# Layer-0 weight products in full fp32 instead of three split-half products

## The reference

```python
def layer0(H, W, A):
    HW = einsum('bnf,fo->bno', H, W)
    A_norm = relu((A + A.T) * 0.5)
    D = sum(A_norm, axis=1)
    d = where(D > 0, D ** -0.5, 0)
    L = eye(N) - d[:, None] * A_norm * d[None, :]
    return relu(einsum('nm,bmo->bno', L, HW))

h = maximum(layernorm(x), 0.0)
x = x + layer0(h, L0_W, adj)
h = maximum(layernorm(x), 0.0)
x = x + layer1(h, L1_W, adj, L1_bias)
```

## Time and profile before

| | |
|---|---|
| median of 3 runs | 978.55 us (977.78 to 979.16) |
| profiled execution, own time | 977.52 us |
| its span, first to last instruction | 975.8 us |
| PE busy | 936.8 us (96%) |
| DVE, ACT, POOL busy | 566.6, 503.6, 287.5 us |
| DMA | 213.73 MB, 219 GB/s on average |

### The profile page before, as it was taken

How to read it: one execution, slowest core, us unless ns; L and a number is a source line. 1 busy time by engine, 2 the same in 40 slices (tenths; PEclk the granted TensorE clock), 3 DMA queues, 4 the chain that set the end, 5 groups by cost and what they waited for, 6 DMA issues and landing times.

```text
span 975.8 us, 17599 instructions
## 1 busy us (share of the span) xinstructions
PE 936.8 (96%) x4614; PEld 796.1 (82%) x4614; DVE 566.6 (58%) x1491; ACT 503.6 (52%) x1058; POOL 287.5 (29%) x289
## 2 busy tenths in 40 slices
PE   4887899999999999999999999999999999999998
PEld 3876688888888888888888887888888888888886
DVE  5885877777777776565665655443443333343442
ACT  5986666666666665545555455433334333333331
POOL 3786143434344343443444433111111100000000
PEclk9977799999999999999999999999999999999999
DMA  8995699999999986566555564676666555555552
GB/s 235 314 327 172 191 299 306 337 313 340 326 310 340 322 285 218 162 175 193 168 171 156 182 194 143 196 217 194 192 184 192 179 168 167 165 167 166 161 164 70
DMA packets 181210, 213.73 MB, mean 219 GB/s; under 512 B 13616, under 2 KB 116016, under 8 KB 178992
## 3 DMA queue, kind: packets, MB, share of 16 engines
q1 hardware_dynamic: 138448, 159.23, 54.0%
q10 hardware_dynamic: 42720, 54.01, 15.8%
HBM read 145.04 MB, written 68.16 MB: 218 GB/s over the span
## 4 chain that ended last, share of the span: by engine, by line
PE 88%; POOL 5%; issue 4%; DMA 1%; DVE 1%; ACT 1%; SPq 0%; ACTq 0%; POOLq 0%; DVEq 0%
PE psAcc L485 23%; PE psAcc L487 23%; PE psAcc L486 23%; POOL colacc L917 3%; PE psA L387 3%; PE psG L456 2%; PE psG L458 2%; PE psG L457 2%; PE psZ L418 2%; POOL n_rs L909 1%; PE psW L359 1%; PE psW L358 1%; PE psAcc L499 1%; PE psAcc L498 1%; PE psAcc L497 1%
## 5 line engine op out<-in xcount | busy, mean ns | idle before, releaser
L545 ACT ACTIVATE Lh<-C 128x512 fp32r<-128x512 f32 x256 | 161.0, 630 | 289.7 <-PE psAcc L487 229.8
L485 PE MATMUL psAcc<-Xh,Lh 128*128 128x512 f32 x512 | 207.7, 406 | 5.6 <-DVE Xl L776 4.7
L487 PE MATMUL psAcc<-Xh,Ll 128*128 128x512 f32 x512 | 202.0, 395 | 0.0
L486 PE MATMUL psAcc<-Xl,Lh 128*128 128x512 f32 x512 | 201.3, 393 | 0.0
L485 PE MATMUL psAcc<-Yh,Lh 128*128 128x512 f32 x512 | 200.8, 392 | 0.0
L487 PE MATMUL psAcc<-Yh,Ll 128*128 128x512 f32 x512 | 200.1, 391 | 0.0
L486 PE MATMUL psAcc<-Yl,Lh 128*128 128x512 f32 x512 | 199.9, 390 | 0.0
L720 DVE TENSOR_TENSOR Ll<-C,Lh 128x512 fp32r<-128x512 f32 x128 | 91.6, 717 | 143.5 <-ACT Lh L545 143.4
L485 PEld LDWEIGHTS psAcc<-Xh,Lh 128*128 128x128 f32 x512 | 97.5, 191 | 24.5 <-issue 6.4
L487 PEld LDWEIGHTS psAcc<-Xh,Ll 128*128 128x128 f32 x512 | 97.1, 190 | 21.2
L487 PEld LDWEIGHTS psAcc<-Yh,Ll 128*128 128x128 f32 x512 | 96.1, 188 | 20.4
(11 more groups left out here) (124 smaller groups left out, 1472.1 us busy)
## 6 DMA issues: line engine op xcount, KB each, us to landing
C<-at_dram SPq DMA_DIRECT2D x128, 256.0 KB, 2.7
at_dram<-AT SPq DMA_DIRECT2D x16, 1088.0 KB, 5.5
R<-in_adj SPq DMA_DIRECT2D x64, 256.0 KB, 6.1
C<-in_adj SPq DMA_DIRECT2D x64, 256.0 KB, 5.3
s_dram<-C ACTq DMA_DIRECT2D x64, 256.0 KB, 4.5
g_dram<-g ACTq DMA_DIRECT2D x32, 512.0 KB, 3.9
C<-s_dram SPq DMA_DIRECT2D x64, 256.0 KB, 3.9
t_dram<-x ACTq DMA_DIRECT2D x32, 256.0 KB, 2.2
```

The lines of the kernel that those rows point to most:

```text
L485: mm(acc, lh, rh[:, k, :], start=k == 0, stop=False)
L486: mm(acc, lh, rl[:, k, :], start=False, stop=False)
L487: mm(acc, ll, rh[:, k, :], start=False, stop=c < L1 and k == NB - 1).then_inc(used, 1)
L545: A(Lh[:, q, :], C[:, q, :], ACT.Relu if s.c < L1 else ACT.Copy).then_inc(lhi, 1)
```

## The change

The transposed tile of `h` stays one fp32 copy, in one of four buffers that are idle in the preparation (`z`, `h2` and the two parts of `g12`). The product with W0 is one fp32 matmul per block, with W0 read as it was loaded (`x1[:, 0, 0:F]`), instead of three fp32r matmuls. The low half on DVE (`low0`) is gone, and with it the semaphore `t0lo`; `t0hi` is now `t0_ok`. ACT's copy may run three tiles ahead of the product instead of one. The second half of the batches keeps its three products (`yTh`, `yTl`).

```diff
-        T0 = [(yTh, yTl), (hTh, hTl)]
+        T0 = [z[:, :], h2[:, :], g12[:, 0, :], g12[:, 1, :]]
...
             def turn0(m):
 
                 pe.wait_ge(s0_h, m + 1)
-                wait(pe, t0hi, m - 1)
-                wait(pe, t0lo, m - 1)
+                wait(pe, t0_ok, m - 1)
...
             def times_W0(m):
 
                 if m == 0:
-                    pe.wait_ge(wlo_ok, 1)
-                pe.wait_ge(t0hi, m + 1)
-                pe.wait_ge(t0lo, m + 1)
+                    pe.wait_ge(ld_w, 32)
+                pe.wait_ge(t0_ok, m + 1)
                 wait(pe, hw0, m - 1)
-                hi, lo = T0[m % 2]
-                by_W0(psG[:, m % 2, :], hi, lo).then_inc(w0_ok, 1)
+                for b in range(HB):
+                    f = slice(b * F, (b + 1) * F)
+                    last = mm(psG[:, m % 2, f], T0[m % 4][:, f], x1[:, 0, 0:F], start=True, stop=True)
+                last.then_inc(w0_ok, 1)
...
                 if c < 2:
-                    pe.wait_ge(t0lo, NB)
+                    pe.wait_ge(t0_ok, NB)
...
                 act.wait_ge(t0, m + 1)
-                wait(act, w0_ok, m - 1)
-                A(T0[m % 2][0][:, :], psAcc[:, m % 2, :], ACT.Copy).then_inc(t0hi, 1)
+                wait(act, w0_ok, m - 3)
+                A(T0[m % 4], psAcc[:, m % 2, :], ACT.Copy).then_inc(t0_ok, 1)
...
                         act.wait_ge(wlo_ok, 1)
+                        act.wait_ge(w0_ok, NB)
...
-            def low0(m):
-                dve.wait_ge(t0hi, m + 1)
-                wait(dve, w0_ok, m - 1)
-                hi, lo = T0[m % 2]
-                V.tensor_tensor(lo[:, :], psAcc[:, m % 2, :], hi[:, :].bitcast(F32), ALU.subtract).then_inc(t0lo, 1)
-
...
-                        if m >= 3:
-                            low0(m - 3)
-            low0(NB - 1)
```

More of the change, by code:

```diff
@@ L169, in build @@
         prep_hi, prep_lo, gpre_lo = sems("prep_hi", "prep_lo", "gpre_lo")
-        t0, t0hi, t0lo, w0_ok, hw0 = sems("t0", "t0hi", "t0lo", "w0_ok", "hw0")
+        t0, t0_ok, w0_ok, hw0 = sems("t0", "t0_ok", "w0_ok", "hw0")
         yT, yThi, yTlo, yw_ok = sems("yT", "yThi", "yTlo", "yw_ok")
```

## The result

| | before | changed |
|---|---|---|
| median of 6 runs | 977.14 us (975.75 to 979.16) | 971.37 us (969.78 to 973.06) |
| ratio, 95% interval | | 0.994 (0.9924 to 0.9957) |
| span of the profiled execution | 975.8 us | 969.1 us |

The kernel is faster by some 5.8 us, 0.6%. When the changed kernel was timed again beside the first experiments, the ratio was 0.9954 (0.9937 to 0.9971), 4.5 us. Single executions of one kernel lie 3 to 4 us apart.

A forecast was written before the change was run, and what follows sets the result against it. Only the preparation, to about 98 us, could gain, with PE full afterwards and no engine full throughout before. 3.4 us by the ring plus 0.86 us at its end gave 4.3 us: 978.55 to 974.3 us, range 971.5 to 977.6 us.

The forecast's parts named there:

- (a): PE, per node tile: four fp32 matmuls replace twelve, eight records, costing 0.9 us less slow and 0.5 us less fast.
- (b): DVE: sixteen low halves removed, 16 x 0.68 = 10.9 us, worth only what somebody waited for.
- the five waits behind the low half: 43 to 75 us: ACT waits at five stages for `sring`, which stands behind the low half on DVE; 2.6 us to gain.
- 17 to 29 us: Early preparation: product starts 1.28 us sooner and is shorter, so ACT becomes last; 2.4 us taken of 2.7 us idle.
- The cap by the loads: Last column strip in the preparation: its landing limits the ring's 5.0 us gain to 3.3 to 5.3 us; 3.4 us taken.
- The ring: Tiles passed round five parties in the preparation: 5.0 us of waits to gain, 3.4 us taken because of the loads.
- The 3.0 us by bytes: 17 to 29 us: how much sooner loads could come, from 253 against 336 GB/s, instead of 1.0 us by DMA share.
- Rival 1: Preparation: loads or POOL hold the ring, worth only 1.3 us there, 976.4 us; chance 0.23 together with the clock rival.
- The end of the preparation: Last node tile's products, before `Xh`: eight records save 0.86 us at the slow clock, all of it on the path.
- rival 2: Column sums: slower clock makes them 6.5 instead of 4.85 us, 975.9 us; chance 0.23 together with the loads-or-POOL rival.

The follow-up runs named there:

- run 5: Changed kernel plus an extra DVE subtraction of the same size at each place where the low half stood, PE not waiting for it: 976.72 us, ratio 0.9989 of before.
- run 2: Kernel before without the low half on DVE, PE still issuing twelve fp32r matmuls per node tile, four buffers: 970.97 us, ratio 0.9943 of before.
- run 3: Kernel before with four fp32 matmuls per node tile, low half still made and waited for, two buffers: 975.21 us, ratio 0.9983 of before.
- run 4: Changed kernel with each fp32 product issued twice: 972.22 us, ratio 0.9955 of before.
- run 8: Kernel before with only half of each column strip loaded in stages 8 to 15: 976.05 us, ratio 0.9988 of before.
- run 1: The changed kernel itself, timed again: 972.53 us, ratio 0.9954 of before.
- run 6: Changed kernel with rings of four instead of three for row and column strips, each load issued a stage sooner: 968.41 us, ratio 0.9916 of before.
- run 7: Changed kernel with only half of each column strip loaded in stages 8 to 15: 970.57 us, ratio 0.9926 of before.
- runs 5 to 10: Includes two more: changed kernel with the fp32 form for the second half too, 966.6 us, ratio 0.989; that with rings of four, 963.16 us, 0.9851.

## Why the prediction was right or wrong

The direction and the place were right: faster, in the preparation, carried to the end by a full PE. The size was put too low. The time fell just below the range, 971.37 us against 971.5 us, and the gain of 4.3 us that was forecast lies below both measured ones, 5.8 and 4.5 us. By its steps:

- **(a), the price of the fp32 product:** right. Eight records at 0.21 and 0.11 us, the lower bound that was taken. The Trainium skill (FP8 and Floating Point Precision, TensorE Precision Notes) counts four passes; the rows show two records, each with its weight load, and 0.89 us a tile, not 1.9. That two passes hide behind each weight load fits this price, but no row shows the passes.
- **(b) and the five waits behind the low half:** right as a mechanism (run 5), and the DVE part alone gives all of the gain (run 2: 0.9943). It is not the only way to some of it: the PE part alone ends the preparation 2.3 us sooner (run 3).
- **"17 to 29 us", where the shorter product was to add its part:** the 2.7 us of ACT's idle time went as forecast, but PE's share in it is worth nothing in the sum as long as a load is last. Run 2 keeps PE's old work and run 4 adds more, and both end the preparation at 80.1 to 80.4 us. What the PE part would be worth with rings of four was not run.
- **"The cap by the loads" is the step that failed.** The ring was to gain 3.4 us: 2.3 us of slack on the last strip, and 1.1 us by which it would land sooner, since the DMA share left a free time of only 1.0 us. Measured are 4.9 us, against a profile of before that may itself be off by 1 us (run 8). PE begins on the last strip 4.4 us sooner (72.53 against 76.93 us), 2.2 us by the slack and 2.2 us by the landing (72.45 against 74.6 us), and behind the strip another 0.5 us goes, for which the sum had no term. In run 1 it is 4.8 us: 2.2, 1.7 and 0.9. A cap it was: PE takes the last strip 0.1 us after it lands, in runs 1, 2 and 4 too, and lighter loads give 3.2 us more. But a share of about 1 was taken for loads that cannot come sooner. When a strip lands is the time at which its slot comes free and some 11 us from issue to landing; the first moves with the ring. Either one slot more (run 6) or fewer bytes in the same slots (run 7) brings the column sums to 77.14 us. The 3.0 us by bytes, which the prediction set aside, was the better measure; with it the cap would have been 5.3 us.
- **Rival 1:** its sign came, PE waits for `colb`, but not its price.
- **The end of the preparation, 0.86 us:** 0.75 us by runs 1, 2 and 3.
- **The clock (rival 2):** the column sums took 3.41, 5.17, 5.24, 6.56 and 3.41 us in the profile after and in runs 1 to 4, and 4.28 to 6.47 us in runs 5 to 10 without run 8. In the profile after, this was a gain of 1.4 us that the forecast did not hold, with 1.0 us more on the way to `Xh`; 1.4 us were lost again before the end, most of it behind `xp`.

Added up for the first profile, whose span fell by 6.7 us: 4.3 forecast, 1.5 more by the ring, 2.4 by the clock before `Xh`, 0.1 less by the last product, 1.4 lost behind it. Between the medians, the forecast of 974.3 us is 2.9 us too high: 1.4 us because the median of before was lower than when it was made, 1.5 us because the gain was larger. Part of that is chance in single executions; in run 1, where the clock gave nothing, the gain was 4.5 us. That this is so near the forecast is partly luck, since the ring gained 1.4 us more than was forecast there too. How much of the difference between 4.5 and 5.8 us is the clock and how much is chance is left open.

## What to carry to other kernels

An instruction whose result nobody waits for can still cost time, if it stands in its engine's order right in front of one that others wait for. A dead instruction put in its place shows that in one run: here sixteen of 0.68 us held the preparation up by 3.2 us. Where engines pass tiles round a ring, relieving one that is not last gives little or nothing: once DVE was relieved, PE's price could double in the preparation without effect. When an engine is relieved, look at what was 2 us early: it is late next. Here one more buffer slot for the loads was worth another 2.3 to 3.7 us.

## What the runs showed of the hardware

A share of the DMA engines of 1.03 did not mean that they were at their limit: with one more slot 342 instead of 313 GB/s went through in the same 15 us, and the last strip landed 3.1 us sooner. One fp32 product of 128 columns is two records, each as dear as one fp32r product of 128 columns (0.11 us at 2.4 GHz, 0.21 us at 1.2 GHz). Against three fp32r products it is a third cheaper on PE. Column sums of one column take as long a record as 128 columns do, 30 of them 3.41 us at the fast and 6.56 us at the slow clock.

DVE's order holds another instruction in front of the low half whose time varies, the small `n_ve` of 128x4. In the kernel before it took 0.17 us at 44.75 us, and 0.90 us at 59.90 us, where it ended (60.80 us) together with POOL's adds (57.30 + 3.47 = 60.77 us):

```profile
44.75 0.17 DVE L701 TENSOR_SCALAR n_ve<-n_mv 128x4 f32<-128x4 f32 x1
...
57.30 3.47 POOL L917 TENSOR_TENSOR colacc<-colacc,sring 128x512 f32<-128x512 f32 x3 [0.93 <-ACT sring L552]
...
59.90 0.90 DVE L701 TENSOR_SCALAR n_ve<-n_mv 128x4 f32<-128x4 f32 x1
```

It is still there after the change. That POOL held it up is not shown by any run, and what its time costs the ring was not tested.
